# Expert scatters that add into two rows per token, each waiting for the one before

## What is computed

```python
scores = softmax(logits)                       # 64 experts
topk_w, topk_idx = top_k(scores, 6)            # 6 experts per token
pos = rank of the token within its expert      # in token order
valid = pos < 64                               # 64 slots per expert, the rest is dropped
d = down(silu(gate(buf)) * up(buf))            # per expert, on its 64 rows
y = sum over the 6 of topk_w * d (0 if dropped)
y = y + shared expert(x);  x = x + y
```

## Time and profile before

| | |
|---|---|
| runs of the kernel | 693.71, 695.05, 695.93 us; median 695.05 us |
| the profiled execution | 695.07 us, its span (first to last instruction) 693.3 us |
| busy share of the span | PE 85%, DVE 74%, ACT 28%, POOL 15% |
| granted TensorE clock, mean | 0.934 of full speed |
| DMA | 114.62 MB, of which 30.15 MB were written to HBM; mean 165 GB/s |
| pair loop | gate/up of pair 0 at 545.6 us, last scatter issued at 648.5 us |
| closing stretch | first load of the sums' rows at 651.0 us, end at 693.3 us |

### The profile page before, as it was taken

One profiled execution on the slowest core, in us unless ns is written; L12 is line 12 of the kernel. 1 busy time (PEld: TensorE's weight loads), 2 busy tenths in 40 slices (PEclk: granted clock), 3 DMA queues, 4 the chain that ended last, 5 costly groups with the idle time before them and its releaser, 6 DMA issues.

```text
span 693.3 us, 7285 instructions
## 1 busy us (share of the span) xinstructions
PE 589.8 (85%) x2297; PEld 334.7 (48%) x2297; DVE 514.0 (74%) x1126; ACT 192.2 (28%) x375; POOL 106.4 (15%) x120
## 2 busy tenths in 40 slices
PE   7569999789998859987889958949599799999865
PEld 6444565435555346543455513534287344444454
DVE  7989888068895859999689996899978355555355
ACT  1112231136432344322543305413110223323000
POOL 2022020300002000020000030000000456664200
PEclk9889999899999959999799977979899999999999
DMA  7960000419102291010750014993071299996497
GB/s 278 405 208 25 16 32 0 134 66 352 43 0 69 93 353 51 23 38 1 282 182 24 1 38 154 348 333 129 0 251 38 77 330 367 373 374 240 178 413 296
DMA packets 50036, 114.62 MB, mean 165 GB/s; under 512 B 6096, under 2 KB 32464, under 8 KB 49488
## 3 DMA queue, kind: packets, MB, share of 16 engines
q1 hardware_dynamic: 42064, 94.36, 38.0%
q0 software_dynamic: 5632, 17.70, 7.3%
q10 hardware_dynamic: 2304, 2.10, 0.9%
HBM read 83.99 MB, written 30.15 MB: 165 GB/s over the span
## 4 chain that ended last, share of the span: by engine, by line
PE 50%; DVE 33%; DMA 6%; issue 4%; ACT 3%; SPq 2%; POOL 1%; DVEq 0%; POOLq 0%; ACTq 0%
PE gate_ps L712 7%; DVE scan_area L1315 7%; PE gate_ps L841 6%; PE up_ps L712 6%; PE misc_ps L729 5%; DMA bc<-part_rows 4%; DVE scan_area L1311 3%; DVE scan_area L1318 3%; PE turn_ps L652 3%; PE ssm_ps L671 3%; PE ssm_ps L761 3%; PE ssm_ps L859 3%; PE misc_ps L812 3%; PE misc_ps L859 3%; SPq L563 2%
## 5 line engine op out<-in xcount | busy, mean ns | idle before, releaser
L1315 DVE TENSOR_TENSOR_SCAN scan_area<-scan_area 128x1024 f32<-128x1024 f32 x32 | 73.3, 2292 | 4.4 <-ACT scan_area L999 0.9
L712 PE MATMUL gate_ps<-big,front_area 128*128 x144 | 74.8, 645 | 1.4 <-ACT front_area L899 1.4
L761 PE MATMUL ssm_ps<-scan_area,ident 128*128 128x512 f32 x128 | 63.5, 629 | 12.6 <-DVE scan_area L1318 11.9
L712 PE MATMUL up_ps<-big,front_area 128*128 x144 | 70.1, 610 | 0.0
L729 PE MATMUL misc_ps<-big,front_area 128*128 x288 | 65.6, 381 | 4.2 <-ACT front_area L899 3.8
L729 PEld LDWEIGHTS misc_ps<-big,front_area 128*128 128x128 f32 x288 | 54.3, 190 | 18.3 <-issue 11.7
L935 ACT ACTIVATE sig<-gate_ps 128x512 f32<-128x512 f32 (+1 forms) x48 | 28.5, 595 | 105.2 <-PE up_ps L712 65.9
L671 PE MATMUL ssm_ps<-zeros,ident 128*128 128x256 f32 x156 | 42.1, 427 | 15.9 <-ACT front_area L899 12.9
L999 ACT ACTIVATE scan_area<-scan_area,a_col 128x511 f32<-128x511 f32 x64 | 42.2, 714 | 39.8 <-DVE scan_area L1315 35.8
L610 POOL DMA_INDIRECT front_area<-ysorted_dram,slot_idx x16 | 18.5, 1155 | 188.0 <-DMA ysorted_dram<-front_area 184.4
L712 PEld LDWEIGHTS up_ps<-big,front_area 128*128 128x128 f32 x144 | 29.0, 201 | 37.9 <-issue 37.9
(11 more groups left out here) (236 smaller groups left out, 904.9 us busy)
## 6 DMA issues: line engine op xcount, KB each, us to landing
bc<-bc_dram SPq DMA_DIRECT2D x4, 4096.0 KB, 13.3
part_rows<-zeros SPq DMA_DIRECT2D x16, 768.0 KB, 15.8
big<-in_wgu SPq DMA_DIRECT2D x15, 704.0 KB
front_area<-in_wgu SPq DMA_DIRECT2D x9, 704.0 KB
big<-part_rows SPq DMA_DIRECT2D x8, 768.0 KB, 9.6
scan_area<-in_wgu SPq DMA_DIRECT2D x6, 704.0 KB
big<-in_wd SPq DMA_DIRECT2D x15, 256.0 KB
front_area<-part_rows SPq DMA_DIRECT2D x5, 768.0 KB, 21.2
```

The lines of the kernel that those rows point to most:

```text
L712: mm = pe.matmul(bank[:], xs_t[:, k, j, :], gu0[:, expert_of[b, j], k, g, half * 512:(half + 1) * 512], start=(k == 0), stop=(k == K - 1))
L761: mm = pe.matmul(ssm_ps[:], ident[:], hs[:, g % HS_RING, n, :], start=False, stop=(g % PER_CHUNK == PER_CHUNK - 1 and n == GROUP - 1))
L1315: nc.vector.tensor_tensor_scan(buf.rearrange(flat), d_a[:, g % 2, :, :].rearrange(flat), buf.rearrange(flat), 0.0, ALU.mult, ALU.add).then ...
```

## The change

A token gets 2 row places in place of 8. A scatter no longer writes its rows: it adds them to what is there. The output for the first expert of a pair goes to the token's row 0, that of the second expert to row 1, so no two rows of one scatter hit the same bytes. Two scatters can, so POOL waits, before it issues the scatter of pair p, for the landing of that of pair p - 1. The gather for pair p + 8 is issued behind the scatter of pair p, as before, and so behind this wait.

With two rows for each token, the clears and the closing loads are 256 KB for a tile in place of 768 KB. PE sums with 2 products in place of 6, DVE with 2 additions in place of 4. In `places` the numbering of a token's choices goes: 4 DVE operations on 256 columns give way to 2 on 128. In `tables` the two copies that make `idx_put` become additions (of 0 or 1 and a constant of 0), and one operation (a minimum, which sends the indices of empty slots to one zero row of the table) is added. The table has 128 zero rows in place of 512, and POOL makes one more constant at the start.

```diff
-PER_TOKEN = 8
-TABLE_ROWS = N + EMPTY // PER_TOKEN
-PART_ROWS = PER_TOKEN * N + EMPTY
+PER_TOKEN = 2
+SETS = PER_TOKEN // 2
+EMPTY_STEP = CAP + PER_TOKEN
+TABLE_ROWS = N + P
+PART_ROWS = PER_TOKEN * N + E * EMPTY_STEP
...
-        part_size = TOPK * D
+        part_size = PER_TOKEN * D
...
-                    sp.dma_start(part_of[b * J + j].rearrange("p (r d) -> p r d", r=TOPK),
-                                 zeros[:, 0:D].unsqueeze(1).broadcast_to([P, TOPK, D])).then_inc(parts_clear, 16)
+                    sp.dma_start(part_of[b * J + j].rearrange("p (r d) -> p r d", r=PER_TOKEN),
+                                 zeros[:, 0:D].unsqueeze(1).broadcast_to([P, PER_TOKEN, D])).then_inc(parts_clear, 16)
...
             for p in range(PAIRS):
                 pool.wait_ge(yo_halves, 2 * (p + 1))
+                if p >= SETS:
+                    pool.wait_ge(rows_put[(p - SETS) % YO_RING], 16 * ((p - SETS) // YO_RING + 1))
                 pool.indirect_dma_start(part_rows, bass.IndirectOffsetOnAxis(idx_put[:, p:p + 1], 0),
-                                        yo[:, p % YO_RING, :], None).then_inc(rows_put[p % YO_RING], 16)
+                                        yo[:, p % YO_RING, :], None, compute_op=ALU.add).then_inc(rows_put[p % YO_RING], 16)
                 if p + ROW_RING < PAIRS:
                     fetch(p + ROW_RING)
...
-                for k in range(TOPK):
+                for k in range(PER_TOKEN):
                     mm = pe.matmul(sum_ps[i], ident[:], parts[i][:, k * D:(k + 1) * D],
-                                   start=(k == 0), stop=(k == TOPK - 1))
+                                   start=(k == 0), stop=(k == PER_TOKEN - 1))
...
-                ts(chosen[:], marked[:, :, 0:E], -3.0, None, ALU.is_equal).then_inc(s, 1)
-                dve.wait_ge(s, b * TOP + 2 * J + 3)
-                flat = chosen[:].rearrange("p j e -> p (j e)")
-                nc.vector.tensor_tensor_scan(nth[:].rearrange("p j e -> p (j e)"), flat, flat, 0.0, ALU.add, ALU.max
-                                             ).then_inc(s, 1)
-                dve.wait_ge(s, b * TOP + 2 * J + 4)
-                stt(out=nth[:], in0=nth[:], scalar=-1.0, in1=wide(tok_value[:, bass.ds(b * J, J)], E),
-                    op0=ALU.mult, op1=ALU.add).then_inc(s, 1)
-                dve.wait_ge(s, b * TOP + 2 * J + 5)
-                by_half = "p (h q) e -> p h q e"
-                tt(placed.rearrange("p (q h e) -> p h q e", q=2, h=2), nth.rearrange(by_half, h=2),
-                   chosen[:].rearrange(by_half, h=2), ALU.mult).then_inc(s, 1)
+                by_half = placed.rearrange("p (q h e) -> p h q e", q=2, h=2)
+                for h in range(2):
+                    at = b * J + 2 * h
+                    stt(out=by_half[:, h, :, :], in0=marked[:, 2 * h:2 * h + 2, 0:E], scalar=-3.0,
+                        in1=wide(tok_value[:, at:at + 2], E), op0=ALU.is_equal, op1=ALU.mult).then_inc(s, 1)
...
-                    nc.vector.tensor_copy(idx_put[rows, :], by_pair[rows, :, e]).then_inc(ids_steps, 1)
+                    stt(out=idx_put[rows, :], in0=by_pair[rows, :, e], scalar=float(e), in1=sum_no[rows, :],
+                        op0=ALU.add, op1=ALU.add).then_inc(ids_steps, 1)
                 dve.wait_ge(ids_steps, 5)
-                ts(idx_get, idx_put, 3, None, ALU.logical_shift_right).then_inc(ids_steps, 1)
+                ts(idx_get.bitcast(I32), idx_put.bitcast(I32), float(PER_TOKEN * TABLE_ROWS - 1), None, ALU.min
+                   ).then_inc(ids_steps, 1)
+                dve.wait_ge(ids_steps, 6)
+                ts(idx_get, idx_get, 1, None, ALU.logical_shift_right).then_inc(ids_steps, 1)
...
-                tt(part[:, 0:half], part[:, 0:half], part[:, half:2 * half], ALU.add).then_inc(part_steps, 1)
-                dve.wait_ge(part_steps, 3 * (i // 2) + 1)
-                tt(part[:, 0:D], part[:, 0:D], part[:, D:2 * D], ALU.add).then_inc(part_steps, 1)
-                tt(xt, xt, part[:, 2 * D:3 * D], ALU.add).then_inc(part_steps, 1)
-                dve.wait_ge(part_steps, 3 * (i // 2) + 3)
-                tt(xt, xt, part[:, 0:D], ALU.add).then_inc(out_ready, 1)
+                tt(xt, xt, part[:, 0:D], ALU.add).then_inc(part_steps, 1)
+                dve.wait_ge(part_steps, i // 2 + 1)
+                tt(xt, xt, part[:, D:2 * D], ALU.add).then_inc(out_ready, 1)
```

More of the change, by code:

```diff
@@ L58 @@
 XW = D + E
-EMPTY = E * CAP
-PER_TOKEN = 8
-TABLE_ROWS = N + EMPTY // PER_TOKEN
-PART_ROWS = PER_TOKEN * N + EMPTY
+PER_TOKEN = 2
[3 more added lines that the diff above has]
+PART_ROWS = PER_TOKEN * N + E * EMPTY_STEP
 YO_RING = 4
@@ L80 @@
 GT = 4
-TOP = 2 * J + 6
+TOP = 2 * J + 4
 ROUNDS = CAP // 8
@@ L143, in build @@
         slot_no = sb("slot_no", [E, CAP])
+        sum_no = sb("sum_no", [P, PAIRS])
         zeros = sb("zeros", [P, XW])
@@ L238, in build @@
         marked = sb("marked", [P, J, E + 2])
-        placed = marked[:].rearrange("p j e -> p (j e)")[:, 0:J * E]
-        chosen = sc
-        nth = att_s[:].rearrange("p r n -> p (r n)")[:, 0:J * E].rearrange("p (j e) -> p j e", j=J)
+        placed = att_s[:].rearrange("p r n -> p (r n)")[:, 0:J * E]
         work = sb("work", [P, CAP + 2 * P])
@@ L286, in build @@
         part_rows = nc.dram_tensor("part_rows", (PART_ROWS, D), F32).ap()
-        part_of = part_rows[0:PER_TOKEN * N, :].rearrange("(i p r) d -> i p (r d)", p=P, r=PER_TOKEN)[:, :, D:D + part_size]
+        part_of = part_rows[0:PER_TOKEN * N, :].rearrange("(i p r) d -> i p (r d)", p=P, r=PER_TOKEN)
         x_loaded = [sem(f"x_loaded{b}") for b in range(B)]
@@ L550, in weights_more @@
                     weights(p)
-            sp.wait_ge(pool_consts, 12)
+            sp.wait_ge(pool_consts, 13)
             run(sp, dict(ffn_load=ffn_load, ffn_out=ffn_out, ssm_proj=ssm_proj, ssm_exp=ssm_exp, places=places,
@@ L579, in _ @@
                                              (last_slot[:], [[-P, J]], SLOTS - 1, -1),
-                                             (tok_value[:], [[-PER_TOKEN * L, B], [TOPK - PER_TOKEN * P, J]],
+                                             (tok_value[:], [[-PER_TOKEN * L, B], [-PER_TOKEN * P, J]],
                                               PER_TOKEN * N, -PER_TOKEN),
@@ L584, in _ @@
                                              (counts_down[:], [[-P, J * (B - 1)]], L * (B - 1), 0),
-                                             (slot_no[:], [[1, CAP]], 0, CAP)):
+                                             (slot_no[:], [[1, CAP]], 0, EMPTY_STEP),
+                                             (sum_no[:], [[0, PAIRS // SETS], [2, SETS]], 0, 0)):
                 nc.gpsimd.iota(dst, pattern, base=base, channel_multiplier=mult,
@@ L623, in tables @@
             def tables(b, _):
-                pool.wait_ge(ids_steps, 6)
+                pool.wait_ge(ids_steps, 7)
                 pool.wait_ge(scratch_clear, 16)
@@ L666, in awake @@
                 if b == 0:
-                    pe.wait_ge(pool_consts, 12)
+                    pe.wait_ge(pool_consts, 13)
                 else:
@@ L1106, in attn_in @@
                 if b == 0:
-                    dve.wait_ge(pool_consts, 12)
+                    dve.wait_ge(pool_consts, 13)
                 norm(0, b, xn_a[b])
@@ L1468, in _ @@
             dve.wait_ge(last_added, 2)
-            half = part_size // 2
             for i in range(0, TILES, 2):
```

## The result

The changed kernel is slower: 746.93 us (median of 4 runs, 744.31 to 748.73) against 695.03 (693.71 to 695.93). The ratio is 1.0746, with a 95% interval of 1.0716 to 1.0776. The profiled execution took 744.31 us, its span 742.5.

The account below looks back on a forecast made before the run. It took the pair loop as PE-bound at 3.08 us, becoming bound by chained scatters: first scatter 552.5, plus 132.8, plus tail 21, gives span 706.3; with 1.8 beside it, 708 us. The 8 in 10 range was 672 to 745.

Parts of the forecast that it names:

- rival D: Pair loop: each scatter far slower, mean period 5 us, time 735 us, at 6 767 us; chance 0.27.
- The mechanism, a chain of landings on POOL that becomes the bound: Pair loop: if the scatter's period, one landing plus POOL's wake, exceeds 3.08 us, all engines fall to it.
- The middle, 3.5: Scatter period in idle DMA time: 3.5 us, between a plain floor of 2.7 and a ceiling of 4.4.
- ceiling of 4.4: Upper limit for the idle scatter period: a same-size gather before the write, one issue shared, plus POOL's wake, 4.4 us.
- 4.8: Scatter period in full DMA time: 4.8 us, from 3.5 plus 1.4 for half a pair's weights standing before it.
- 8.1 us store: Nearest row for a loaded ceiling: a finished tile's 128 KB store under the sum loads, 8.1 us to landing.
- 16 scatters in full time, 16 in idle: Pair loop: weights flow up to about scatter 15, so 16 scatters at 4.8 us and 16 at 3.5, together 132.8 us.
- The tail of 21: Closing stretch, DMA-bound: 21 us in place of 42.3, a gain of 21.3 from 8.39 MB less.
- `places`, 4 us: Numbering of choices: two smaller DVE operations let PE turn 1.1 to 1.5 us sooner in 3 batches, gain 4 us.
- Clears and `tables`, 0: Fewer clears go out in DMA time nothing awaits, and the added table operation's 0.3 us is covered: 0 each.
- Late gathers: Pair loop: the gather stands behind POOL's wait but 8 pairs ahead, so DVE's weighing feels a late landing first.
- Rival A: Pair loop: the chain is hidden, mean period under 3.15 us, time 673 us; chance 0.13.

Follow-up runs that it names:

- The wait alone: Kernel before, with each plain scatter also waiting for the landing of the last pair's scatter, still 8 row places per token: 740.24 us, ratio 1.0654.
- without the stream: Changed kernel without the weights' loads of pairs 12 to 31, which are computed with weights already in the ring: 723.55 us, one run.
- two sets: Changed kernel with 4 rows per token, even and odd pairs apart, a scatter waiting for that of the pair before the last: 701.40 us, ratio 1.0099.
- adding alone: Kernel before, with scatters that add in place of writing, 8 places per token and no added wait: 699.99 us, ratio 1.0049.
- the swap: POOL's wait for the last scatter's landing put before that for the weighing: 731.55 us in the kernel before with the added wait, 738.72 in the changed kernel.

## Why the prediction was wrong

The direction was right, the size was not: 746.93 against 708, just above the range's 745. What came is rival D in its mean period, 170.3 / 32 = 5.3 us (I had given D a chance of 0.27 and 735 at 5).

- **The mechanism, a chain of landings on POOL that becomes the bound: right.** The wait alone makes 45.6 us of it, the chain that ended last is made of it, and without the stream the loop falls to near what the idle period gives. With two sets it shortens too, by 56 us, though less than I expected.
- **"The middle, 3.5" for an idle period: the step that failed.** It measured 4.57, above even my ceiling of 4.4. Taken apart: the issue is 1.55 us in place of 0.96 (+0.6); from its end to the landing 3.83 - 1.55 = 2.3 in place of 2.41 - 0.96 = 1.45 (+0.8); POOL's restart is 0.73 in place of 0.27 (+0.46). I took the ceiling from a gather and a write one after the other with a plain issue, so that both adding's issue and the restart lay outside it. The restart was in a row, but the wrong one: 0.27 follows a single wait, for DVE. The issue of 1.58 us is also one of the signs of being wrong that the prediction names ("well over 0.98 us").
- **"4.8" for a loaded period: too small, but through the 3.5 in it.** It measured 5.94 ((646.59 - 551.63)/16). What the forecast adds to the idle period for load, 4.8 - 3.5 = 1.3, measured 5.94 - 4.57 = 1.37. With 4.57 and this same 1.3, 16 x 5.87 + 16 x 4.57 are 167 us, of the 170.3 measured. That the 1.3 fits is in part luck: the plain chain has 5.20 - 3.15 = 2.05 for it, and nothing tests that half of a pair's weights stand before a scatter. I discounted the 8.1 us store because a longer period empties the queues. That does happen: the DMA share falls from 1.00 to 0.84, and of the landings only the second and third take 8 us, the median of the first 16 is 4.7 (4.5 in the plain chain). That the scatters of adding alone land after 8.1 us, as the store did, is chance: another queue, another stretch, a plain write.
- **16 scatters in full time, 16 in idle: right.** The last weights were issued at 644.91, and the 17th scatter started at 646.59. The periods make the whole error: 16 x 5.94, 15 x 4.76 (4.57 and a few late ones) and the last landing of 3.9 are 170.3, against 132.8, 37.5 us; the span is 742.5 against 706.3, 36.2.
- **The tail of 21: right,** 20.6 us, with DMA at a share of 0.92. The 2.2 us in its floor run from the end of the last addition (691.02 to 693.3); from its start, as the text has it, they are 2.7.
- **`places`, 4 us: right where it can be read.** DVE's 1.94 us of the earlier trace rows became 0.51, here in the first batch, and PE's turn follows:

```profile
252.25 0.51 DVE att_s L1371 x2
252.76 0.14 issue
252.89 1.51 PE turn_ps L655 x6
```

  That is 1.4 us. PE's waits for it, 15.7 us in three batches, are now 11.3 in two, 4.4 less; in the second batch PE no longer waits:

```profile
  DVE att_s L1371: 11.3, 2
```

  The first scatter came 4.9 earlier, but this start moves by some us between executions of one kernel: the first gather starts at 540.3 to 544.5 in five profiles with the old `places`, mean 542.8, and at 537.3 to 543.9 in eight with the new one, mean 539.2. The difference of 3.6 agrees.
- **Clears and `tables`, 0: nothing speaks against it,** and no run tells them apart from the variation of the start.
- **Late gathers, which I had called covered: right in the sum,** though one of them (6.19 us, at 613.70) does stand in the chain that ended last. To send them first gave 3.5 us, which POOL's shorter restart accounts for.
- **Rival A, a hidden chain, needed a period under 3.15.** Even the plain one is 3.15 with the waits in this order. With the landing's wait first it is 2.67, and would be hidden, in idle DMA time alone.

What stays open: why POOL's restart depends on which of two waits is the late one (shown by the swap in a plain and in an adding kernel, with no record of what it does in those 0.5 us); what an adding scatter does in its 0.6 us more of issue and 0.8 us more to landing; and what share of the loaded landing is queueing behind weights and what is slower memory. No run here separates these.

## What to carry to other kernels

Before a wait for the landing of the last transfer is put into a loop, multiply the number of passes by the whole latency from that engine's issue to its own restart, taken under the load of that loop. An overlap of up to four transfers hides latencies of 8 us that a chain pays one by one; bytes saved in a later stretch (here 21.7 us) must be set against that. If the chain must be, put the wait that ends last first, and give it a second set of targets.

## What the runs showed of the hardware

- An indirect scatter that adds takes POOL 1.58 us to issue against 0.98, and lands 3.8 us after its start against 2.4 in idle DMA time. Next to a gather of 0.99 it makes POOL's beat 3.18 us.
- For 128 rows of 1 KB it has 96 more packets than a plain one, and takes 0.47 us more of all 16 DMA engines in the mean of the loop; in idle DMA time 1.15 us against 0.38.
- Adding scatters of 131 KB, two or three in flight at a beat of 3.18 us, land 8.1 us after their start in the median when weights stream beside them, at 351 GB/s in all. Chained one after the other, they take 4.7 us in the median of the changed kernel's first half.
- POOL starts an indirect DMA mostly 0.27 us after a late wait that has a met one behind it, or that stands alone, and 0.73 to 0.78 us after a late wait that has a met one ahead of it.
